# Query splits of layer 2 on VectorE instead of GpSimd, repeated parts copied by ScalarE, and a remade order of steps, in a two-layer transformer kernel

## The chip, the core and the metric

The kernel is one program on one core of a Trainium2 chip. A core has five engines that run their own instruction streams side by side and wait for one another through semaphores: TensorE (PE, matrix products and transposes into PSUM; PEld are its weight loads), VectorE (DVE), ScalarE (ACT), GpSimd (POOL), and SyncE (SP), which here only issues transfers. The metric is the device time of one execution in microseconds, lower is better. The kernel before was timed three times, with a median of 364.91 us (364.82 to 368.45).

## What is computed

Two batches of 512 tokens with 128 features go through a cross attention with a residual, a mixture of experts, a second cross attention, and a block with self attention and gated experts. Cut to what matters here (16 heads of 8 dimensions everywhere; the context has 77 tokens):

```python
x = x + xattn0(layernorm(x), ctx)                 # softmax(q k^T / sqrt(8)) v, projection
x = x + moe0(layernorm(x))                        # 8 experts, top 2: relu(x w1)^2 w2
x = x + xattn1(ctx, layernorm(x))                 # softmax(q k^T) v, + residual, layer norm
# block 2: self attention with rotary q, k over 512 keys
q = rope(src @ Wq); k = rope(src @ Wk_c @ Wk); v = src @ Wv_c @ Wv
x = rmsnorm(src + softmax(q k^T / sqrt(8)) v @ Wo)
shared = swiglu(x @ W_shared_in) @ W_shared_out
routed = sum_e (swiglu(x @ W1_shared) @ W2[e]) * w[:, e]     # grouped top-2 gates
out = rmsnorm(x + shared + routed)
```

## The kernel before

Everything stays in on-chip memory after the loads at the start. Work is cut into steps, written out by hand in one list, `ORDER`. Each engine walks this list and runs its own part of each step, so the list sets the order on every engine at once; what it does not set are the waits, which semaphores enforce. A step's first number is the layer (0 and 1 cross attention, 2 self attention), or, where there is none, the batch.

The steps that matter here:

- `QP`, `KV` and `CKV` project queries and keys. `SPLITQ`, `SPLITK` and `SPLITC` cut each float32 value into three bfloat16 parts (a high part, the rest's high part, and what is left), so that scores can be formed from bfloat16 products without losing accuracy. A row of `qcat` or `kcat` holds six slots of 8 numbers for each head. `Q_PART = (0, 0, 1, 1, 0, 2)` and `K_PART = (0, 1, 0, 1, 2, 0)` say which part stands in which slot: the first part three times, the second twice, the third once. So each split is two casts, two subtractions and three plain copies of a part to its further slots.
- `QT`, `KT` and `KTC` transpose `qcat` and `kcat` on TensorE, and ScalarE or VectorE copies the result out of PSUM (each takes one half of the tokens).
- `SMAX layer group part half` forms scores on TensorE, and VectorE takes their maximum (line 1112). `MCH` splits the maxima (GpSimd in layers 0 and 2, VectorE in layer 1), `MTR` transposes them. `ST` forms the transposed scores less the maximum, and ScalarE takes the exponential (line 896). In layer 1 a further step, the guard, clamps the exponentials (line 545 on GpSimd, line 1120 on VectorE). `PV` is the product with the values, `OC` and `OTR` bring it out.
- `FH` and `FY` are an expert's two products in block 0; `STAT` and `NORM` are normalizations, whose reciprocal root (a power) is always taken by GpSimd; `GH`, `SO`, `RO`, `GT`, `GTE` are the experts and gates of block 2.

PSUM is used as a ring of three large buffers (`ring_ps`), one small one (`misc_ps`) and one for attention outputs (`out_ps`). The ring's buffers are given out in the order of the list, so a step of TensorE waits until the step three places earlier on the ring has been read. `BORROWING` lists small steps that use the ring in place of `misc_ps`.

In layers 0 and 1 and for all keys, the split runs on VectorE (`split`, lines 1016 to 1028). The queries of layer 2 are split by GpSimd (`POOL_SPLITS`, lines 547 to 567), in its own copy of the code and with its own buffer for the rest (`RSP`).

## Time and profile before

| | profile before |
|---|---|
| median of three runs | 364.91 us |
| the profiled execution, its own time | 368.39 us |
| its span, first to last instruction | 366.6 us |
| mean granted TensorE clock | 0.884 of full speed |
| PE busy | 308.5 us (84%) |
| DVE busy | 278.8 us (76%) |
| ACT busy | 203.0 us (55%) |
| POOL busy | 92.0 us (25%) |
| chain that ended last | PE 57%, DVE 21%, issue 10%, ACT 7%, POOL 3% |

The stages follow one another in the span roughly so: loads and the first projections until 20 us, cross attention of layer 0 until 62, experts of block 0 (with the first batch of layer 1 woven in) until 145, the second batch of layer 1 and the first keys and queries of layer 2 until 184, self attention until 305, and the experts of block 2 to the end.

How to read it: an engine's share of busy time is an average over these stages, and in each of them another engine can be the one that the others wait for. The granted clock is the share of its 2.4 GHz that TensorE was given: 1.00 is 2.4 GHz, 0.50 is 1.2 GHz, and a value between is a stretch with some of both. The profiled execution took 3.48 us more than the median.

### The profile page before, as it was taken

How to read it: one execution, taken by the hardware profiler on the slowest of the kernel's cores; microseconds unless marked ns; L12 is line 12 of the kernel's file. 1: busy time of each engine (PE TensorE's matmuls, PEld its weight loads, DVE VectorE, ACT ScalarE, POOL GpSimd, SP SyncE). 2: the span in 40 equal slices, each digit the busy share in tenths (PEclk: the TensorE clock that was granted, in tenths of full speed). 3: DMA queues.
4: the chain of work that ended last, by engine and by line, in shares of the span. 5: the costliest groups of instructions: out<-in, count | busy, mean ns of one | idle time of the engine just before them, and what ended most of it. 6: DMA issues, size and time to landing. Idle time of an engine off the chain costs nothing.

```text
span 366.6 us, 5813 instructions
## 1 busy us (share of the span) xinstructions
PE 308.5 (84%) x2146; PEld 162.5 (44%) x2146; DVE 278.8 (76%) x703; ACT 203.0 (55%) x242; POOL 92.0 (25%) x144
## 2 busy tenths in 40 slices
PE   1679899999998996584877859889889999999990
PEld 0553565577685753572721114242223233745530
DVE  2886667643588968879799699897999851887985
ACT  3245658656664785346452646875779998501200
POOL 4322131010110364319825143911111020011001
PEclk9995889999999999567585587998999999999996
DMA  7910000000000000000000000000000000000000
GB/s 221 431 70 0 2 3 1 2 0 3 0 2 0 2 3 0 0 2 0 2 0 1 3 0 0 2 2 0 2 0 1 2 2 1 0 2 0 30 0 30
DMA packets 1900, 7.48 MB, mean 20 GB/s; under 512 B 208, under 2 KB 336, under 8 KB 1488
## 3 DMA queue, kind: packets, MB, share of 16 engines
q1 hardware_dynamic: 1872, 7.11, 5.2%
q8 instruction: 17, 0.28, 0.3%
q14 instruction: 11, 0.09, 0.1%
HBM read 6.58 MB, written 0.52 MB: 19 GB/s over the span
## 4 chain that ended last, share of the span: by engine, by line
PE 57%; DVE 21%; issue 10%; ACT 7%; POOL 3%; DMA 1%; POOLq 0%; SPq 0%; ACTq 0%; DVEq 0%
PE ring_ps L578 30%; PE out_ps L578 13%; DVE mx L1112 10%; PE ring_ps L674 3%; ACT pT L896 3%; PE misc_ps L578 2%; PE misc_ps L709 2%; ACT qT L880 2%; PE misc_ps L759 1%; ACT hid L924 1%; PE ring_ps L709 1%; DVE Z L960 1%; DVE X L1288 1%; PE misc_ps L595 1%; PE ring_ps L664 1%
## 5 line engine op out<-in xcount | busy, mean ns | idle before, releaser
L896 ACT ACTIVATE pT<-ring_ps 128x1024 f32<-128x1024 f32 (+1 forms) x96 | 94.5, 1025 | 35.3 <-PE ring_ps L578 33.2
L1112 DVE TENSOR_REDUCE mx<-ring_ps 128x2 f32<-128x1024 f32 (+1 forms) x96 | 99.5, 1076 | 13.9 <-PE ring_ps L578 13.1
L506 POOL TENSOR_TENSOR rstd<-var,consts 128x4 f32<-128x4 f32 x14 | 14.7, 1051 | 122.1 <-DVE var L982 62.0
L578 PE MATMUL ring_ps<-XT,f 128*128 128x512 f32 x96 | 44.8, 602 | 0.6 <-ACT hid L924 0.3
L578 PE MATMUL out_ps<-pT,V 128*32 128x512 f32 x256 | 39.8, 666 | 0.0
L545 POOL TENSOR_SCALAR pT<-pT 77x1024 f32<-77x1024 f32 x8 | 23.0, 2880 | 36.4 <-ACT pT L896 36.4
L578 PE MATMUL ring_ps<-f,hid 128*128 128x512 f32 (+1 forms) x96 | 31.8, 487 | 0.0
L578 PEld LDWEIGHTS ring_ps<-f0y,hid 128*128 128x128 f32 x256 | 29.7, 192 | 3.8 <-issue 3.1
L578 PE MATMUL ring_ps<-f0y,hid 128*128 128x128 f32 x256 | 30.9, 277 | 0.1
L578 PE MATMUL ring_ps<-qT,kT 51*128 51x512 bf16 x128 | 24.7, 412 | 6.9 <-DVE mx L1112 3.6
L1288 DVE SCALAR_TENSOR_TENSOR X<-ring_ps,gw,X 128x128 f32<-128x128 f32 x64 | 18.0, 344 | 16.1 <-PE ring_ps L578 15.9
L578 PE MATMUL ring_ps<-kT,qT 48*128 48x512 bf16 x128 | 25.5, 424 | 3.7 <-DVE mx L1112 2.7
L533 POOL TENSOR_SCALAR qcat<-mx 128x16 bf16<-128x16 f32 x16 | 5.3, 330 | 85.9 <-DVE mx L1112 75.8
L578 PEld LDWEIGHTS ring_ps<-XT,f 128*128 128x128 f32 x96 | 17.0, 190 | 18.4 <-issue 15.5
L924 ACT ACTIVATE hid<-ring_ps 128x1024 f32<-128x1024 f32 x16 | 16.3, 1017 | 14.0 <-PE ring_ps L578 14.0
L578 PE MATMUL out_ps<-pT,Vc 77*32 77x512 f32 x128 | 21.7, 720 | 1.6 <-POOL pT L545 1.5
L674 PE MATMUL ring_ps<-identb,qcat 128*128 128x128 bf16 x192 | 17.7, 274 | 5.7 <-DVE qcat L960 5.6
L1288 DVE SCALAR_TENSOR_TENSOR ACC<-ring_ps,gw,ACC 128x128 f32<-128x128 f32 x64 | 19.5, 347 | 3.4 <-PE ring_ps L578 2.4
L578 PEld LDWEIGHTS ring_ps<-f,hid 128*128 128x128 f32 x96 | 15.7, 191 | 14.4 <-issue 14.3
L880 ACT COPY qT<-ring_ps 128x2048 bf16<-128x2048 bf16 x6 | 11.2, 1866 | 18.4 <-PE ring_ps L674 18.4
L578 PE MATMUL ring_ps<-qT,kTc 51*77 51x512 bf16 x64 | 14.5, 485 | 7.0 <-DVE mx L1112 4.4
L674 PEld LDWEIGHTS ring_ps<-identb,qcat 128*128 128x128 bf16 x192 | 16.5, 127 | 7.8 <-DVE qcat L960 6.7
(185 smaller groups left out, 459.1 us busy)
## 6 DMA issues: line engine op xcount, KB each, us to landing
f<-in_f SPq DMA_DIRECT2D x1, 1669.0 KB, 15.2
f<-in_f SPq DMA_DIRECT2D x1, 1028.0 KB, 8.4
f0y<-in_f0y SPq DMA_DIRECT2D x1, 1024.0 KB, 10.4
X<-in_x SPq DMA_DIRECT2D x2, 256.0 KB, 4.5
wb<-in_wb SPq DMA_DIRECT2D x1, 512.0 KB, 11.2
rows<-in_rows SPq DMA_DIRECT2D x1, 512.0 KB, 11.4
trig<-in_trig SPq DMA_DIRECT2D x1, 512.0 KB, 12.0
out<-ACC SPq DMA_DIRECT2D x2, 256.0 KB, 2.0
```

What stands on the lines that cost most here:

```text
L506: return pool.tensor_tensor(out, a, c, op)
L533: pool.tensor_scalar(c[:, :, :, 0], m, -1.0, None, ALU.mult)
L545: pool.tensor_scalar(heads, heads, 0.0, None, ALU.max).then_inc(done["GUARD"], 1)
L578: return nc.tensor.matmul(out, lhsT, rhs, start=start, stop=stop)
L595: last = nc.tensor.transpose(small_ps(step)[:, t * P:(t + 1) * P], source[kind][b][:, t, :], ident)
L674: last = nc.tensor.transpose(ps[:, t, p * P:(p + 1) * P], qcat[b][:, 2 * u + t, p, :], identb[:, :])
L709: last = nc.tensor.transpose(ps[:, a * N + t * P:a * N + (t + 1) * P], qcat[b][:, t, 2 * g + a, :], identb[:, :])
L880: nc.scalar.copy(dst, src).then_inc(ring.read_sem(step), 1)
L896: nc.scalar.activation(probs_buf(layer, i, kt)[0:parts_, 2 * half:2 * half + 2, :], ring_ps[ring.buf(step)][0:parts_, :, :], ACT.Exp, scal ...
L924: nc.scalar.activation(relu[n % 2], src, ACT.Relu).then_inc(ring.read_sem(step), 1)
L1112: V_.tensor_reduce(dst, src, AX.X, ALU.max).then_inc(ring.read_sem(step), 1)
L1288: return V_.scalar_tensor_tensor(out=acc[:, t, :], in0=src, scalar=w, in1=acc[:, t, :], op0=ALU.mult, op1=ALU.add)
```

## The change

- `POOL_SPLITS` is empty: the queries of layer 2 are split by VectorE in the same `split` as all others.
- `split` no longer makes the three copies. It signals after each of its two casts (`PART`), and ScalarE makes the copies in new steps `DUPQ`, `DUPK` and `DUPC`: one instruction of two slots for the first part and one of one slot for the second. There are ten such steps, one for each split. The transposes `QT`, `KT` and `KTC` wait for them as well as for the split.
- `ORDER` and `BORROWING` are written anew. All steps are kept, the ten new ones are put in, and nearly every step stands a few places away from where it was.

```diff
-POOL_SPLITS = {(2, 0), (2, 1)}
+POOL_SPLITS = set()
...
-    STAT n0 0, NORM n0 0, STAT n0 1, XT n0 0, QP 0 0, SPLITQ 0 0, NORM n0 1, CKV 0, SPLITC 0, QT 0 0 0, QT 0 0 1,
+    STAT n0 0, NORM n0 0, CKV 0, SPLITC 0, XT n0 0, QP 0 0, SPLITQ 0 0, DUPQ 0 0, STAT n0 1, DUPC 0, KTC 0 0,
...
             def QT(step, layer, b, u):
 
                 pe.wait_ge(*after("SPLITQ_POOL" if (layer, b) in POOL_SPLITS else "SPLITQ", layer, b))
+                pe.wait_ge(*after("DUPQ", layer, b))
...
+            def copies(split_step, cat, first, heads, part_of, parts=P):
+
+                for k in range(2):
+                    act.wait_ge(*after("PART", *split_step, k))
+                    at = [s for s, part in enumerate(part_of) if part == k]
+                    size = int(np.prod(cat.shape[1:]))
+                    n, gap = len(at) - 1, 3 * DH
+                    out = bass.AP(cat, first * HS + at[1] * DH, [[size, parts], [HS, heads], [gap, n], [1, DH]])
+                    src = bass.AP(cat, first * HS + at[0] * DH, [[size, parts], [HS, heads], [0, n], [1, DH]])
+                    last = nc.scalar.copy(out, src)
+                return last
+
+            def DUPQ(step, layer, b):
+                copies(("SPLITQ", layer, b), qcat[b], 0, T * H, Q_PART).then_inc(done["DUPQ"], 1)
...
-                link(V_.tensor_copy(dst(s0), flat_heads(values)))
+                V_.tensor_copy(dst(s0), flat_heads(values)).then_inc(done["PART"], 1)
+                dve.wait_ge(*after("PART", *step, 0))
                 link(tt(flat_heads(rest), flat_heads(values), dst(s0), ALU.subtract))
-                link(V_.tensor_copy(dst(s1), flat_heads(rest)))
-                for s, k in enumerate(part_of):
-                    if k < 2 and s != (s0, s1)[k]:
-                        V_.tensor_copy(dst(s), dst((s0, s1)[k]))
+                V_.tensor_copy(dst(s1), flat_heads(rest)).then_inc(done["PART"], 1)
+                dve.wait_ge(*after("PART", *step, 1))
                 return tt(dst(s2), flat_heads(rest), dst(s1), ALU.subtract)
```

Three places show what the new list does on an engine. Line numbers of the changed kernel are 6 to 30 higher.

**On TensorE, at the last experts of block 0.** `f0y,hid` is an expert's second product (`FY`), `XT1,f0` its first (`FH`), `qT0,kTc10` the transposed scores of layer 1 (`ST`), `pT,Vc10` the product with the values. Before:

```order
L578 MATMUL ring_ps2<-XT1,f0 128x512 x2
L578 MATMUL out_ps<-pT1,Vc10 32x512 x4
L578 MATMUL ring_ps0<-f0y,hid 128x128 x8
L709 MATMUL misc_ps<-identb,qcat0 128x128 x8
L578 MATMUL ring_ps1<-qT0,kTc10 77x512 x2
L578 MATMUL ring_ps2<-f0y,hid 128x128 x8
L578 MATMUL ring_ps0<-qT0,kTc10 77x512 x2
L578 MATMUL ring_ps1<-wb 128x256
L578 MATMUL ring_ps2<-qT0,kTc10 77x512 x2
L578 MATMUL out_ps<-pT0,Vc10 32x512 x4
```

After the change:

```order
L718 MATMUL ring_ps0<-identb,qcat0 128x128 x8
L584 MATMUL ring_ps1<-XT1,f0 128x512 x2
L584 MATMUL ring_ps2<-f0y,hid 128x128 x8
L584 MATMUL ring_ps0<-qT0,kTc10 77x512 x2
L584 MATMUL out_ps<-pT1,Vc10 32x512 x4
L584 MATMUL ring_ps1<-qT0,kTc10 77x512 x2
L584 MATMUL ring_ps2<-qT0,kTc10 77x512 x2
L584 MATMUL ring_ps0<-f0y,hid 128x128 x8
L584 MATMUL ring_ps1<-qT0,kTc10 77x512 x2
L584 MATMUL out_ps<-pT0,Vc10 32x512 x4
```

The scores of the fourth group, first half (`ST 1 3 0 0`, the row ahead of `wb` before), now stand ahead of the last expert's product instead of behind it, and the transposed maxima (line 709) moved up past two expert products.

**On VectorE, at the first keys and queries of layer 2.** `kcat` and `qcat0` are the split keys and queries, `KF0` and `ACC0` their float32 values, `mx2` and `mx3` maxima of layer 1. Before:

```order
L960 TENSOR_TENSOR KF0<-KF0,Z0 128x512
L1022 CAST kcat<-KF0 128x64x8
L960 TENSOR_TENSOR Z0<-KF0,kcat 128x512
L1024 CAST kcat<-Z0 128x64x8
L1027 COPY kcat<-kcat 128x64x8 x3
L960 TENSOR_TENSOR kcat<-Z0,kcat 128x64x8
L1120 TENSOR_SCALAR pT0<-pT0 77x1024
L1120 TENSOR_SCALAR pT1<-pT1 77x1024
L1112 TENSOR_REDUCE mx3<-ring_ps0 128x2x4
```

After the change:

```order
L991 TENSOR_TENSOR KF0<-KF0,Z0 128x512
L1142 TENSOR_REDUCE mx3<-ring_ps1 128x2x4
L1053 CAST kcat<-KF0 128x64x8
L991 TENSOR_TENSOR Z0<-KF0,kcat 128x512
L1056 CAST kcat<-Z0 128x64x8
L991 TENSOR_TENSOR kcat<-Z0,kcat 128x64x8
L1053 CAST qcat0<-ACC0 128x64x8
L991 TENSOR_TENSOR Z0<-ACC0,qcat0 128x512
L1056 CAST qcat0<-Z0 128x64x8
L991 TENSOR_TENSOR qcat0<-Z0,qcat0 128x64x8
L1150 TENSOR_SCALAR pT0<-pT0 77x1024
L1121 COPY kT0<-ring_ps1 128x2x8x128
```

The three copies are gone, the four operations of the query split came in, one maximum moved ahead of both, and the second guard moved behind.

**On TensorE, at the first products with the values of layer 2.** `kT0,qT0` are scores for the maxima (`SMAX`), `qT0,kT0` the transposed ones (`ST`), `pT,V0` the products with the values (`PV`). Before:

```order
L578 MATMUL ring_ps2<-qT0,kT0 128x512 x2
L578 MATMUL ring_ps0<-qT0,kT0 128x512 x2
L578 MATMUL out_ps<-pT0,V0 32x512 x4
L578 MATMUL out_ps<-pT1,V0 32x512 x4
L578 MATMUL ring_ps1<-kT0,qT0 128x512 x2
L578 MATMUL ring_ps2<-kT0,qT0 128x512 x2
```

After the change:

```order
L584 MATMUL out_ps<-pT1,Vc11 32x512 x4
L584 MATMUL ring_ps0<-kT0,qT0 128x512 x2
L584 MATMUL ring_ps1<-qT0,kT0 128x512 x2
L584 MATMUL ring_ps2<-qT0,kT0 128x512 x2
L584 MATMUL out_ps<-pT0,V0 32x512 x4
L584 MATMUL ring_ps0<-kT0,qT0 128x512 x2
L584 MATMUL ring_ps1<-qT0,kT0 128x512 x2
L584 MATMUL out_ps<-pT1,V0 32x512 x4
```

Scores for the maxima now stand between the first two products with the values; before, both products stood ahead of the next such score.

## Rows read from the trace of the kernel before

**Rows 1.** Busy time by stretch: us; busy and count by engine; granted clock; DMA.

```profile
145.00:168.00 23.00, 15.59 (x138) 12.66 (x138) 19.21 (x55) 10.64 (x19) 6.37 (x7) 0.63 0.00 1
...
168.00:184.00 16.00, 10.40 (x94) 7.75 (x94) 13.64 (x28) 7.86 (x7) 13.84 (x8) 0.57 0.00 1
...
188.00:212.00 24.00, 17.64 (x80) 3.72 (x80) 20.13 (x39) 12.31 (x15) 8.74 (x9) 0.57 0.00 1
...
225.00:268.00 43.00, 38.22 (x302) 14.38 (x298) 38.46 (x45) 32.62 (x34) 14.74 (x22) 0.96 0.00 1
...
268.00:305.00 37.00, 35.49 (x265) 11.33 (x266) 28.34 (x45) 33.00 (x37) 4.86 (x16) 1.00 0.00 1
...
305.00:356.00 51.00, 51.00 (x186) 25.92 (x184) 39.11 (x147) 14.09 (x17) 2.01 (x2) 1.00 0.02 6
...
sum 366.60, PE 308.48 PEld 162.45 DVE 278.76 ACT 203.01 POOL 92.00; mean PE 25.71 PEld 13.54 DVE 23.23 ACT 16.92 POOL 7.67
```

**Rows 2.** Timeline, 136.9 to 145: start us, duration, engine, what, [idle before].

```profile
136.92 2.05 PE L578 MATMUL ring_ps<-f0y,hid 128*128 128x128 f32 x16
...
140.51 2.76 POOL L545 TENSOR_SCALAR pT<-pT 77x1024 f32<-77x1024 f32 x1 [3.58 <-ACT pT L896]
...
141.88 0.16 DVE L978 TENSOR_SCALAR var<-mv 128x4 f32<-128x4 f32 x1
...
143.25 1.46 POOL L506 TENSOR_TENSOR rstd<-var,consts 128x4 f32<-128x4 f32 x1
...
145.02 1.65 ACT L844 ACTIVATE XN<-X,shift,rstd 128x128 f32<-128x128 f32 x4 [3.05 <-POOL shift L506]
```

**Rows 3.** Groups of VectorE and ScalarE instructions by line and shape.

```profile
L1027 DVE COPY qcat<-qcat 128x512 bf16<-128x512 bf16 x12 | 3.7, 367 | 0.1
...
L1027 DVE COPY kcat<-kcat 128x512 bf16<-128x512 bf16 x6 | 2.5, 468 | 0.1
...
L1027 DVE COPY kcat<-kcat 77x256 bf16<-77x256 bf16 x6 | 1.0, 219 | 0.1
...
L1022 DVE CAST qcat<-ACC 128x512 bf16<-128x512 f32 x4 | 1.7, 424 | 0.1
...
L1022 DVE CAST kcat<-KF 128x512 bf16<-128x512 f32 x2 | 1.2, 606 | 0.0
...
L960 DVE TENSOR_TENSOR Z<-ACC,qcat 128x512 f32<-128x512 f32 x4 | 2.8, 692 | 0.1
...
L888 ACT COPY qT<-misc_ps 128x1024 bf16<-128x1024 bf16 x14 | 14.1, 1008 | 7.2 <-PE misc_ps L709 7.2
...
L908 ACT COPY oT<-out_ps 128x512 f32<-128x512 f32 x16 | 9.4, 588 | 7.1 <-PE out_ps L578 6.9
```

**Rows 4.** Timeline, 172 to 184: keys and queries of layer 2, batch 0.

```profile
172.37 1.52 DVE L1027 COPY kcat<-kcat 128x512 bf16<-128x512 bf16 x3
...
174.39 1.71 POOL L506 TENSOR_TENSOR qcat<-RSP,qcat 128x512 bf16<-128x512 f32 x1
...
177.50 1.87 PE L664 MATMUL ring_ps<-identb,kcat 128*128 128x128 bf16 x16 [1.07 <-DVE mx L1112]
...
179.16 3.62 PE L674 MATMUL ring_ps<-identb,qcat 128*128 128x128 bf16 x32
...
182.82 1.22 DVE L1099 COPY qT<-ring_ps 128x2048 bf16<-128x2048 bf16 x1 [1.45 <-PE ring_ps L674]
```

**Rows 5.** Timeline, 210.6: VectorE's longest wait in layer 2.

```profile
210.57 8.01 DVE L1112 TENSOR_REDUCE mx<-ring_ps 128x2 f32<-128x1024 f32 x7 [3.23 <-PE ring_ps L578]
```

**Rows 6.** Timeline, 238 to 245: queries of layer 2, batch 1.

```profile
238.65 1.15 POOL L506 TENSOR_TENSOR qcat<-RSP,qcat 128x512 bf16<-128x512 f32 x1
...
241.89 1.07 PE L674 MATMUL ring_ps<-identb,qcat 128*128 128x128 bf16 x16
...
243.00 1.87 ACT L880 COPY qT<-ring_ps 128x2048 bf16<-128x2048 bf16 x1 [1.77 <-PE ring_ps L674]
```

**Rows 7.** Timeline, 357: the last sums of experts.

```profile
357.25 2.55 DVE L1288 SCALAR_TENSOR_TENSOR ACC<-ring_ps,gw,ACC 128x128 f32<-128x128 f32 x8 [0.89 <-PE ring_ps L578]
```

More of the change, by code:

```diff
@@ L381, in after @@
                 return done[kind], same.index(("OTR",) + args) + 1
+            if kind == "PART":
+                on_pool = args[:1] == ("SPLITQ",) and args[1:3] in POOL_SPLITS
+                same = [s for s in splits if (s[0] == "SPLITQ" and s[1:] in POOL_SPLITS) == on_pool]
+                return done["PARTP" if on_pool else "PART"], 2 * same.index(args[:-1]) + args[-1] + 1
             if kind == "QROT":
@@ L397, in build @@
         hidden = [s[1:] for s in schedule if s[0] == "FH"]
+        splits = [s for s in schedule if s[0] in ("SPLITQ", "SPLITK", "SPLITC")]
         maxes = [s[1:3] for s in schedule if s[0] == "SMAX" and s[3:] == (0, 0)]
@@ L560, in SPLITQ @@
                 s0, s1, s2 = (Q_PART.index(k) for k in range(3))
-                link(copy(dst(s0), values))
+                copy(dst(s0), values).then_inc(done["PARTP"], 1)
+                pool.wait_ge(*after("PART", *step, 0))
                 link(tt(rest, values, dst(s0), ALU.subtract))
-                link(copy(dst(s1), rest))
-                for s, k in enumerate(Q_PART):
-                    if k < 2 and s != (s0, s1)[k]:
-                        copy(dst(s), dst((s0, s1)[k]))
+                copy(dst(s1), rest).then_inc(done["PARTP"], 1)
+                pool.wait_ge(*after("PART", *step, 1))
                 tt(dst(s2), rest, dst(s1), ALU.subtract).then_inc(done["SPLITQ_POOL"], 1)
@@ L651, in KTC @@
                 pe.wait_ge(*after("SPLITC", layer))
+                pe.wait_ge(*after("DUPC", layer))
                 wait_free(ring, step)
@@ L659, in KT @@
                 pe.wait_ge(*after("SPLITK", b))
+                pe.wait_ge(*after("DUPK", b))
                 wait_free(ring, step)
@@ L1015, in CKV, with split @@
                 last.then_inc(misc.read_sem(step), 1)
-            def split(cat, first, pairs, values, rest, part_of, parts=P):
+            def split(step, cat, first, pairs, values, rest, part_of, parts=P):
                 def dst(s):
@@ L1033, in SPLITC @@
                 flatr = kr[0:C, :, :].rearrange("p b d -> p (b d)")
-                split(kcat, 2 * layer * H, B * H, flatk, flatr, K_PART, C).then_inc(done["SPLITC"], 1)
+                split(step, kcat, 2 * layer * H, B * H, flatk, flatr, K_PART, C).then_inc(done["SPLITC"], 1)
             def rotate(src, out, tmp):
```

114 lines of the change are left out of this document (60 added, 54 removed).

## Prediction

> **What bounds the kernel now.** I read the busy time by stretch first [rows 1], since the shares of the whole span mix stages. TensorE is busy for 308.48 of 366.60 us, but not evenly. From 305 to 356 us it is busy for all 51.00, and from 268 to 305 for 35.49 of 37, at a granted clock of 1.00. There the end is set by TensorE's work, and no other engine's relief helps. From 145 to 212 it is different. Between 168 and 184 TensorE is busy for 10.40 of 16 us while VectorE is busy for 13.64, and between 188 and 212 for 17.64 of 24 against VectorE's 20.13. The granted clock in both is 0.57, that is mostly 1.2 GHz, after stretches in which TensorE waited. So the middle of the kernel is paced by VectorE and by waits, and it costs twice, once as idle time and once as a slow clock. A change of this kind must earn its time there.
>
> Second came the timeline around the hand-over from block 0 to layer 1 [rows 2]. GpSimd clamps exponentials from 140.51 to 143.27, and the statistics that it should turn into the reciprocal root were ready at 142.04 (141.88 and 0.16). The root starts at 143.25, the normalization that hangs on it at 145.02. All work of the second batch of layer 1 follows from it.
>
> Third, the prices of the operations that move [rows 3], and fourth, the two places where the queries of layer 2 are made [rows 4, 6].
>
> **The change, part by part.**
>
> *Copies taken off VectorE.* The 24 copies of a part are 3.7, 2.5 and 1.0 us of VectorE, 7.2 in all [rows 3]. For one query split that is 3.7/4 = 0.9 us. A further gain is indirect: the cast of keys takes 606 ns and that of queries 424 for the same shape. The keys of layer 2 are cast while GpSimd works on the queries, so I put the difference down to that, and it goes with the GpSimd split. It is 0.18 us for each cast.
>
> *Query splits put on VectorE.* Each is two casts and two subtractions, 2 x 0.424 + 2 x 0.692 = 2.2 us [rows 3], so 4.4 us for two. VectorE thus does 7.2 - 4.4 = 2.8 us less in all, plus some tenths.
>
> *Copies put on ScalarE.* The trace has no copy within SBUF on this engine. The nearest rows are its copies out of PSUM, 1.01 us for 1024 elements and 0.59 for 512 [rows 3]. A query or key pair is one of each, so 1.6 us. Six query pairs and two key pairs are 12.8 us, and the two context pairs about 1.6 us more (0.6 and a little less for half of it): some 14 us. From below I take the 512-element price for both (9.4 us for the eight), from above 3 us for a pair if the short runs of 8 elements cost double. I take 1.6, since the rows have the same size and type.
>
> The Trainium skill, "ScalarE: Activation LUTs" (Rules for kernel authors), says plain elementwise operations belong on VectorE, which is up to about 3 times faster for one source in bf16. The trace agrees with its direction, and by it the trade is a loss wherever ScalarE is the one waited for. That is the slower rival below.
>
> *Layer 0.* On the path of a split, ScalarE's second copy can start after the second cast and ends (0.59) with VectorE's last subtraction (0.69), so where ScalarE is free the transposes start 0.9 us earlier. In the experts' stage TensorE covers it. In layer 0 I take 0.9 us for one of the two batches (the other's copies stand behind exponentials and context copies). **-0.9**, bounds 0 and -1.8.
>
> *The root behind the clamp.* The new order puts those scores ahead of the last expert product of 2.05 us, so the clamp ends before the statistics are ready, and the root can start at 142.04 instead of 143.25 [rows 2]. **-1.2**, bounds 0 (if the exponentials ahead of it are late) and -2.05.
>
> *Keys and queries of layer 2, batch 0.* VectorE loses the key copies (1.52 us here [rows 4]) and 0.36 for slower casts, and gains 2.2, net +0.3. GpSimd ends the split at 176.10, but TensorE takes up these transposes only at 179.16, because it is busy with the keys' until 179.37 [rows 4]. So GpSimd's slowness was hidden, and taking it away gains nothing by itself. The keys could start earlier now. But ScalarE's two pairs (3.2 us) are waited for; it is busy for only 7.86 of 16 us there [rows 1], so they fit. **0**, bounds -1.5 (the copies that went) and +2.2.
>
> *VectorE's wait of 3.23 us before 210.57* [rows 5]. It comes from two products with the values in a row, with no scores for a maximum between them. The new order puts scores there. But exponentials, products and transposed maxima now stand together a little later, and there VectorE may wait anew. I take half, **-1.6**, bounds 0 and -3.23.
>
> *Keys and queries of layer 2, batch 1.* Here GpSimd ends at 239.80 and TensorE starts the transposes at 241.89 [rows 6], so again it was hidden. VectorE's sum is even (+2.2, -1.25, some tenths). ScalarE gets two pairs in a row, 3.2 us, ahead of its two transposed halves of 1.87. It is busy for 32.62 of 43 us here and 33.00 of 37 right behind [rows 1]. Behind the copies wait the exponentials, behind these the products with the values, and TensorE for a free ring buffer. It idles for 10.4 us in the stretch, so most is absorbed. **+1.0**, bounds 0 and +3.2.
>
> *The end.* The second batch's gates come later in the new order. VectorE now waits 0.89 us before the last experts' sums [rows 7], so lateness up to that is free. **+0.2**, bounds 0 and +1.0. The silu steps move between exponentials, but the number of table loads stays at four, and TensorE has its own work beside them.
>
> The sum is -0.9 - 1.2 + 0 - 1.6 + 1.0 + 0.2 = -2.5 us. The profiled execution took 368.39, so it would take 365.9. It lay 3.48 above the median of 364.91, which therefore goes to **362.4 us**. All bounds at once would be 364.91 - 8.6 = 356.3 and 364.91 + 6.4 = 371.3.
>
> **The rivals.**
>
> *The clock holds (0.20).* The sum leaves TensorE's clock as it was. In 168 to 184 and 188 to 212 TensorE is busy for 28.0 us at 0.57 [rows 1]; at 1.00 this work would take 12.0 us less (28.0 x 0.43). For it speaks that both the longest wait of VectorE and the wait for the root go, and with them some of TensorE's idle time ahead of these stretches. Against it speaks that VectorE is busy for 20.13 of 24 us, so a faster TensorE mostly waits for it. A third of 12.0 gives -4, and with the sum above **358.4 us**. The Trainium skill, "TensorE: Matmul & The Clock Gate" (Part 1), says that the clock is throttled by default and released by activity. The trace agrees: 1.00 in the dense stretch behind 268, 0.57 in the two with waits.
>
> *Nothing comes of it (0.18).* The GpSimd split was hidden in both batches [rows 4, 6], and each new order trades one wait for another. Then VectorE's waits come back a few steps later, and the time is **365 us**, between 363.5 and 366.5.
>
> *ScalarE becomes the bound (0.22).* The mechanism is the queue at the keys and queries of layer 2: two pairs of copies there, 3.2 us in each batch, stand ahead of transposed halves and exponentials, so that TensorE stalls for a ring buffer. It decides if the idle time of ScalarE near the copies is less than the 3.2 us that they take, though the stretch as a whole has 10.4. With both pairs paid in full and the wait before 210.57 not gained the sum is -0.9 - 1.2 + 3.2 + 3.2 + 0.2 = +4.5, so **369.4 us**. For it speaks that ScalarE is busy for 33.00 of 37 us behind the second place. Against it: half the time idle at the first.
>
> **How the numbers follow.** The forecast above has 0.40, with a range of its own from 360.0 to 364.6. A measurement of this kernel can tell about 1% from no change, that is below 361.3 or above 368.6. Faster by over 1%: the clock's 0.20, and 0.18 of the forecast's 0.40, 0.38 in all. Slower by over 1%: most of ScalarE's 0.22, 0.20. The rest, 0.42, is no change: 0.22, 0.18 and 0.02. For 8 in 10 the range must reach to the clock's case and into ScalarE's: 356.3, where all bounds at once lie, is more than needed, so 356.5 to 369.0.
>
> **What would show it.** In the profile of the changed kernel:
> - ScalarE's copies within SBUF at about 1.0 and 0.6 us, ScalarE near 217 us busy, VectorE near 275, and GpSimd's 92.00 us down by its two splits.
> - The root behind the last clamp starts within 0.3 us of its statistics. If it waits for the clamp again, the term of -1.2 is wrong.
> - VectorE's longest wait for scores in layer 2 is under 2 us. If one of 3 us stands elsewhere, the term of -1.6 is wrong.
> - Exponentials right behind the copies of batch 1 wait for ScalarE itself and TensorE idles for under 1 us there. If it idles for 3, the slower rival holds.
> - The granted clock between 145 and 228 stays near 0.6. If it is above 0.8, the clock's rival holds.
>
> The prediction as a whole is wrong if TensorE's idle time in layers 1 and 2 grows, or if a place that I did not look at, such as layer 0 with its new order, changes by more than 2 us.

## The result and the profile after

The changed kernel takes 366.69 us (median of 20 executions) against 364.91 for the one before (20, on the same chip). Their ratio is 1.0052, with a 95% interval from 1.0033 to 1.0071. It is slower, by about half a per cent, where 362.4 was forecast. The range of 356.5 to 369.0 holds it.

All ratios below compare a kernel with the one before on the same chip. 0.1% is 0.365 us, and "+1.9 us" for a ratio of 1.0052 is worked out so. The ratios are not those of the medians and leave out executions over 1.5% above the fastest of their kernel, so the two can differ by up to 1.8 us (e1: +5.3 by the ratio, +7.1 by the medians).

The page of the changed kernel: busy time by engine, then the granted clock in 40 slices, in tenths.

```profile
span 365.7 us, 5806 instructions
...
PE 305.4 (84%) x2146; PEld 160.4 (44%) x2146; DVE 273.6 (75%) x687; ACT 217.1 (59%) x262; POOL 70.7 (19%) x130
...
PEclk9978999999999996667675589999899999999997
```

ScalarE has 14.1 us more, as forecast (217), and VectorE 5.2 less, where 275 would have been 3.8 less. The span is 0.9 us shorter than the one shown of before, although the medians say 1.8 longer. That execution of before lay 3.48 above its median, this one 0.78. A second profile of the unchanged kernel (below) serves as the comparison.

Busy time by stretch, columns as in [rows 1]:

```profile
20.00:62.00 42.00, 37.19 (x408) 21.83 (x406) 30.90 (x72) 29.41 (x41) 12.57 (x43) 0.92 0.01 5
...
145.00:168.00 23.00, 13.54 (x136) 11.00 (x136) 19.02 (x43) 11.10 (x17) 3.54 (x6) 0.68 0.00 1
168.00:184.00 16.00, 11.78 (x108) 8.56 (x108) 12.45 (x24) 10.87 (x11) 3.27 (x2) 0.68 0.00 1
...
188.00:212.00 24.00, 19.31 (x92) 3.66 (x92) 20.50 (x30) 9.22 (x10) 5.85 (x9) 0.53 0.00 1
...
225.00:268.00 43.00, 36.91 (x288) 14.61 (x288) 38.64 (x47) 33.16 (x38) 3.83 (x15) 0.96 0.00 1
268.00:305.00 37.00, 36.03 (x251) 12.79 (x250) 27.92 (x47) 32.16 (x36) 4.81 (x16) 1.00 0.01 1
305.00:356.00 51.00, 50.23 (x192) 24.34 (x190) 38.75 (x145) 13.97 (x16) 2.02 (x2) 1.00 0.02 6
```

Against [rows 1] the middle looks alike: TensorE idles for 9.5 us from 145 to 168 (7.4 before), and its clock from there to 212 is 0.53 to 0.68 in the long stretches. The rival in which the clock holds did not come about. The end is TensorE's as before.

The root behind the clamp, timeline at 132 to 140 (to be held against [rows 2]):

```profile
131.99 6.02 POOL L552 TENSOR_SCALAR pT<-pT 77x1024 f32<-77x1024 f32 x2 [2.90 <-ACT pT L926]
...
136.91 0.16 DVE L1009 TENSOR_SCALAR var<-mv 128x4 f32<-128x4 f32 x1
...
137.98 1.46 POOL L513 TENSOR_TENSOR rstd<-var,consts 128x4 f32<-128x4 f32 x1
...
139.75 1.65 ACT L853 ACTIVATE XN<-X,shift,rstd 128x128 f32<-128x128 f32 x4 [2.23 <-POOL shift L513]
```

The statistics are ready at 137.07 and the root starts at 137.98, right behind a clamp that ends at 138.01. It waits 0.91 us, where it waited 1.21.

Keys and queries of layer 2, batch 0 (against [rows 4]):

```profile
166.18 1.03 ACT L926 ACTIVATE pT<-ring_ps 77x1024 f32<-77x1024 f32 x1
...
167.30 2.77 POOL L552 TENSOR_SCALAR pT<-pT 77x1024 f32<-77x1024 f32 x1 [14.10 <-ACT pT L926]
167.34 1.28 DVE L1053 CAST kcat<-KF 128x512 bf16<-128x512 f32 x1
168.65 1.04 ACT L878 COPY kcat<-kcat 128x1024 bf16<-128x1024 bf16 x1 [1.43 <-DVE kcat L1053]
...
169.38 0.97 DVE L1056 CAST kcat<-Z 128x512 bf16<-128x512 f32 x1
170.38 0.62 ACT L878 COPY kcat<-kcat 128x512 bf16<-128x512 bf16 x1 [0.69 <-DVE kcat L1056]
...
171.13 3.59 PE L672 MATMUL ring_ps<-identb,kcat 128*128 128x128 bf16 x32 [4.36 <-DVE kcat L991]
...
175.03 1.94 PE L584 MATMUL out_ps<-pT,Vc 77*32 77x512 f32 x8
...
176.90 3.41 PE L683 MATMUL ring_ps<-identb,qcat 128*128 128x128 bf16 x32
...
180.35 1.22 DVE L1129 COPY qT<-ring_ps 128x2048 bf16<-128x2048 bf16 x1 [2.34 <-PE ring_ps L683]
```

GpSimd's split is gone, but one of its clamps now lies beside VectorE's casts of the keys. They take 1.28 and 0.97 us, where I had counted 0.42 for each. TensorE idles 4.36 us for the keys. ScalarE's copies have the forecast prices, 1.04 and 0.62. The new list also has a product with the values (175.03) ahead of the queries' transposes, where the old list has it behind them, and VectorE waits 2.34 us for these.

Batch 1, ScalarE's queue (against [rows 6]):

```profile
235.61 4.70 ACT L926 ACTIVATE pT<-ring_ps 128x1024 f32<-128x1024 f32 x5
240.14 1.60 ACT L878 COPY qcat<-qcat 128x1024 bf16<-128x1024 bf16 x2
241.59 1.61 ACT L878 COPY kcat<-kcat 128x1024 bf16<-128x1024 bf16 x2
...
241.84 1.95 PE L683 MATMUL ring_ps<-identb,qcat 128*128 128x128 bf16 x32 [1.73 <-ACT qcat L878]
...
243.06 1.92 ACT L910 COPY qT<-ring_ps 128x2048 bf16<-128x2048 bf16 x1
...
243.83 1.23 DVE L1129 COPY qT<-ring_ps 128x2048 bf16<-128x2048 bf16 x1 [1.53 <-PE ring_ps L683]
```

The parts of the queries were ready at 238.78 (a cast of 0.43 from 238.35), but ScalarE reached the first copy only at 240.14, behind five exponentials in a row. It makes four copies in 3.06 us. TensorE idles 1.73 us for those of the queries, between the 1 and the 3 that the prediction had named as signs, and VectorE then waits 1.53 for the transposes.

VectorE's waits from 180 to 250, in all, times, longest:

```profile
DVE mx L1142 <- PE ring_ps L584: 4.6, 6, 2.1
DVE qT L1129 <- PE ring_ps L683: 3.9, 2, 2.3
DVE oT L1185 <- PE out_ps L584: 1.1, 2, 0.8
```

The wait of 3.23 [rows 5] is gone, and in its place stand six waits for scores of 4.6 us together, and 3.9 for queries. The last sums of experts [rows 7] start at 356.32 with a wait of 0.53.

Ends of steps on VectorE, from the traces (us). Below, *early* is up to the statistics of layer 2's first input, *batch 0* from there to the last copied query of layer 2's batch 0, *batch 1* to the first maximum of group 4 in layer 2, *end* the rest. "Last row" is the end of VectorE's last operation:

| kernel | statistics | batch 0 queries | group 4 | last row | early | batch 0 | batch 1 | end |
|---|---|---|---|---|---|---|---|---|
| before, second profile | 156.48 | 183.09 | 249.23 | 361.22 | 156.5 | 26.6 | 66.1 | 112.0 |
| after | 151.82 | 181.57 | 250.75 | 363.17 | 151.8 | 29.8 | 69.2 | 112.4 |

So the changed kernel is 4.7 us ahead at layer 2's statistics, gives back 3.1 at batch 0 and 3.0 at batch 1, and loses 0.4 at the end. These are two single executions; the medians say 1.8, these say 1.95.

### The profile page after: what moved, and what is told of

Read it like the earlier page. It is cut to its first block, busy times and chain, and to the rows that moved or that the text cites. A ratio compares the mean times of both kernels' runs of the same rounds, so it can differ in the third digit from the quotient of the medians.

```text
span 365.7 us, 5806 instructions
## 1 busy us (share of the span) xinstructions
PE 305.4 (84%) x2146; PEld 160.4 (44%) x2146; DVE 273.6 (75%) x687; ACT 217.1 (59%) x262; POOL 70.7 (19%) x130
## 4 chain that ended last, share of the span: by engine, by line
PE 57%; DVE 20%; issue 10%; ACT 8%; POOL 3%; DMA 1%; POOLq 0%; SPq 0%; ACTq 0%; DVEq 0%
PE ring_ps L584 28%; PE out_ps L584 12%; DVE mx L1142 10%; PE ring_ps L683 4%; PE misc_ps L584 4%; ACT pT L926 3%; POOL pT L552 2%; PE ring_ps L718 2%; PE ring_ps L672 2%; PE misc_ps L768 1%; DMA wa<-in_wa 1%; DVE Z L991 1%; PE misc_ps L718 1%; ACT qcat L878 1%; PE misc_ps L601 1%
## 5 line engine op out<-in xcount | busy, mean ns | idle before, releaser
L926 ACT ACTIVATE pT<-ring_ps 128x1024 f32<-128x1024 f32 (+1 forms) x96 | 94.8, 1024 | 29.7 <-PE ring_ps L584 25.3
L584 PE MATMUL ring_ps<-XT,f 128*128 128x512 f32 x96 | 43.9, 598 | 0.0
L584 PE MATMUL out_ps<-pT,V 128*32 128x512 f32 x256 | 38.6, 651 | 0.0
L584 PE MATMUL ring_ps<-kT,qT 48*128 48x512 bf16 x128 | 26.4, 437 | 5.4 <-DVE mx L1142 3.8
L683 PE MATMUL ring_ps<-identb,qcat 128*128 128x128 bf16 x192 | 16.2, 260 | 7.6 <-DVE qcat L991 4.6
L584 PEld LDWEIGHTS ring_ps<-kT,qT 48*128 48x128 bf16 x128 | 5.9, 96 | 31.7 <-issue 13.7
L683 PEld LDWEIGHTS ring_ps<-identb,qcat 128*128 128x128 bf16 x192 | 15.1, 121 | 10.4 <-issue 5.3
L959 ACT ACTIVATE hid<-hid 128x1024 f32<-128x1024 f32 x16 | 16.9, 1057 | 3.1 <-PE ring_ps L584 2.7
```

The source lines that it names most:

```text
L584: return nc.tensor.matmul(out, lhsT, rhs, start=start, stop=stop)
L683: last = nc.tensor.transpose(ps[:, t, p * P:(p + 1) * P], qcat[b][:, 2 * u + t, p, :], identb[:, :])
L926: nc.scalar.activation(probs_buf(layer, i, kt)[0:parts_, 2 * half:2 * half + 2, :], ring_ps[ring.buf(step)][0:parts_, :, :], ACT.Exp, scal ...
L959: nc.scalar.activation(h2[n % 2][:, :, :].rearrange("p c n -> p (c n)"), relu[n % 2], ACT.Square).then_inc(done["FH"], 1)
```

## The experiments

Ratios, intervals and medians (e0 has one execution, 365.51 us). "Old" and "new" order are those of before and of the changed kernel. *Early* covers layers 0 and 1 up to the query transposes of layer 1's second batch (`QT 1 1 1`).

| | early: order, copies | layer 2: order, splits of queries, copies | median | ratio to before (95%) |
|---|---|---|---|---|
| before | old, VectorE | old, GpSimd, with the split | 365.4 | 1 |
| e4 | old, ScalarE | old, GpSimd, with the split | 366.57 | 1.0037 (1.0011 to 1.0063) |
| e2 | old, ScalarE | old, GpSimd, ScalarE | 371.23 | 1.0186 (1.0147 to 1.0224) |
| e1 | old, ScalarE | old, VectorE, ScalarE | 372.54 | 1.0146 (1.0100 to 1.0192) |
| e3 | new, VectorE | new, GpSimd, with the split | 371.74 | 1.0153 (1.0115 to 1.0192) |
| e10 | new, ScalarE | new, GpSimd, with the split | 371.01 | 1.0129 (1.0077 to 1.0180) |
| e5 | new, ScalarE | new, VectorE, VectorE | 365.33 | 1.0000 (0.9966 to 1.0034) |
| after | new, ScalarE | new, VectorE, ScalarE | 366.69 | 1.0052 (1.0033 to 1.0071) |
| e6 | new, ScalarE | as the changed kernel, one clamp more on VectorE | 368.53 | 1.0073 (1.0039 to 1.0107) |
| e11 | new, VectorE | old, GpSimd, with the split | 363.83 | 0.9937 (0.9897 to 0.9977) |
| e7 | new, ScalarE | old, GpSimd, with the split | 361.99 | 0.9914 (0.9882 to 0.9946) |
| e15 | the same again | | 361.75 | 0.9905 (0.9873 to 0.9938) |
| e12 | new, ScalarE | old; batch 0 as e7; batch 1 VectorE, VectorE | 362.01 | 0.9899 (0.9859 to 0.9939) |
| e14 | new, ScalarE | old; as e7, batch 0's key copies ScalarE | 361.48 | 0.9856 (0.9796 to 0.9917) |
| e8 | new, ScalarE | old, VectorE, VectorE | 364.40 | 0.9980 (0.9947 to 1.0013) |
| e16 | new, ScalarE | old, VectorE; copies: batch 0 ScalarE, 1 VectorE | 362.31 | 0.9918 (0.9889 to 0.9946) |
| e17 | new, ScalarE | old; batch 0 as e7; batch 1 VectorE, ScalarE | 365.58 | 1.0019 (1.0003 to 1.0035) |
| e9 | new, ScalarE | old, VectorE, ScalarE | 366.52 | 0.9995 (0.9960 to 1.0031) |
| e13 | new, ScalarE | old, VectorE, ScalarE, batch 0 behind exponentials | 366.68 | 1.0023 (0.9983 to 1.0064) |

### The two halves of the change: e0 to e3

e0 is the kernel before, unchanged.

> The kernel before, unchanged, for a second profile of it. The first one was 368.39 us where the median is 364.91, and its granted clock from 20 to 62 us was 0.80. If the clock of a single execution makes this gap, this execution lies near 365 us, its clock in that stretch is nearer to 0.9, and VectorE's busy time is the same 276 us within 1.

It took 365.51 us, with a clock of 0.84 from 20 to 62 us instead of 0.80. So 2.9 of the 3.48 us by which the first profile lay high were that one execution. They are not lost in that stretch: at the statistics of layer 2's first input the two profiles are 0.1 us apart. They arise behind it, where the granted clock from 145 to 305 us was 0.84 instead of 0.81.

e1 has the old list with the new steps put in. The second query split had to be moved up, since VectorE would otherwise wait for its own later step.

```diff
-    MTR 1 5, SPLITK 0, SPLITQ 2 0, ST 1 4 0 0, ST 1 4 0 1, ST 1 5 0 0, ST 1 5 0 1, SMAX 1 7 0 0, SMAX 1 7 0 1, KT 0 0,
+    MTR 1 5, SPLITK 0, DUPK 0, SPLITQ 2 0, DUPQ 2 0, ST 1 4 0 0, ST 1 4 0 1, ST 1 5 0 0, ST 1 5 0 1, SMAX 1 7 0 0,
...
-    PV 2 1 3, SPLITK 1, SMAX 2 3 0 1,
+    PV 2 1 3, SPLITK 1, DUPK 1, SPLITQ 2 1, DUPQ 2 1, SMAX 2 3 0 1,
```

> The order and the borrowed buffers of before, with both engine changes: the query splits of layer 2 on VectorE and all copies of parts on ScalarE, each right behind its split. Theory A (the engine change gains, the remade order loses): 363 to 364 us, 0.3 to 0.5% under the kernel before. Theory B (the copies queued on ScalarE at the keys and queries of layer 2 cost more than GpSimd's relief gives, and the remade order only repairs that): 367 to 369 us. Theory C (neither matters, waits trade places): 365 within 0.7.

e2 is the same with GpSimd's splits kept (`DUPQ 2 1` then stands behind `KT 1 1`):

```diff
-POOL_SPLITS = set()
+POOL_SPLITS = {(2, 0), (2, 1)}
```

> The order of before, copies of parts on ScalarE, but the query splits of layer 2 still on GpSimd. It holds one half of the engine change alone. Theory A: near 364.5, since the GpSimd split was hidden and only the copies matter, and they are taken off VectorE (-0.9 in layer 0). Theory B: 366 to 368, since the queue of copies on ScalarE is all there. Theory C: 365 within 0.7.

e3 is the kernel before with the new list and borrowed buffers, without the `DUP` steps.

> The remade order and borrowed buffers, with the engines of before: query splits of layer 2 on GpSimd, copies of parts on the engine that splits. Theory A (the order loses): 367 to 369 us, more than the changed kernel's 366.7. Theory B (the order gains about 1 to 2 by the root and the wait of 3.23 us): 363 to 364. Theory C: 365 within 0.7. In layer 2 VectorE now has the copies within a queue laid out without them, so up to 1.5 us more than this at each of the two places is possible under all three.

Each half alone costs 1.5%, 5.3 us for both engine changes in the old order (e1) and 5.6 for the order (e3); the copies alone, without VectorE's query splits, cost 6.8 (e2). Order and engines together cost 0.5%. Theory B was right in kind on the copies, though they cost more than it said (+6.8 in e2), and wrong on the order. A was right on the order and wrong on the engines. The new order is laid out for a quick query split, and with GpSimd's VectorE waits 5.2 us for those queries (e3, VectorE's waits from 170 to 192):

```profile
DVE qT L1098 <- PE ring_ps L673: 5.2, 1, 5.2
```

### Where each part pays: e4 to e7

e4 has ScalarE's copies in layers 0 and 1 only. `DVE_COPIES` names the splits that make their own copies as before:

```diff
+DVE_COPIES = {('SPLITK', 1), ('SPLITQ', 2, 0), ('SPLITQ', 2, 1), ('SPLITK', 0)}
...
                 dve.wait_ge(*after("PART", *step, 1))
+                if step in DVE_COPIES:
+                    for s, k in enumerate(part_of):
+                        if k < 2 and s != (s0, s1)[k]:
+                            V_.tensor_copy(dst(s), dst((s0, s1)[k]))
```

> The order of before; copies of parts on ScalarE in layers 0 and 1 only. Layer 2 stays as in the kernel before: its query splits on GpSimd, its copies behind the splits on the engine that splits. Theory Q (the copies queue ahead of exponentials at the keys and queries of layer 2; in the trace of the kernel with all copies on ScalarE in this order VectorE's step lay 3.6 us later behind the first place and 3.2 behind the second): nearly all of that kernel's +5.8 us is there, so this one lies within 1.5 us of before, 364.0 to 367.0 us. Theory R (the loss is the clock or layers 0 and 1): 369 us or more.

+1.4 us, against +6.8 with layer 2's copies on ScalarE too. So in the old order 5.4 of the 6.8 are layer 2's. Theory Q holds.

e5 is the changed kernel with the same `DVE_COPIES` and without layer 2's four `DUP` steps.

> The changed kernel, with the copies of layer 2's parts (four pairs of keys and queries) put back on VectorE behind their splits; query splits stay on VectorE, copies of layers 0 and 1 on ScalarE. Theory Q (ScalarE's queue is what costs in the changed kernel too): 364 to 366 us, faster than its 366.7, since 6.4 us of ScalarE go and 5 us of VectorE come at places where ScalarE was queued. Theory O (the new order is fitted to ScalarE's copies, and VectorE is on the path there): about 1 us for each of the four pairs, 369 to 371 us.

1.9 us less than the changed kernel. The intervals touch, so it points to Q and rules out O's 369 to 371. In its profile batch 0, batch 1 and end (as in the table of steps) are 28.5, 68.8 and 111.2 us, against 29.8, 69.2 and 112.4 in the changed kernel. So of its gain only 0.4 us lies in batch 1.

e6 puts one clamp on VectorE:

```diff
-DVE_GUARDS = {(i, 1) for i in range(NGRP)}
+DVE_GUARDS = {(i, 1) for i in range(NGRP)} | {(4, 0)}
```

> The changed kernel, one clamp more on VectorE: the first half of layer 1's group 4, which GpSimd clamps from 167.30 to 170.07 us while VectorE casts the keys. The casts took 1.28 and 0.97 us there, against 0.42 without GpSimd beside them. Theory P (a running GpSimd operation slows VectorE's casts): both casts take 0.4 to 0.5 us, the keys' split is 1.4 us shorter, VectorE pays 0.68 for the clamp, and the kernel gains 0.5 to 1, 365.7 to 366.3 us. Theory N (casts are slow there for another reason): the casts stay above 0.9 and the kernel is 0.7 slower, 367.4.

368.53 us, 1.0073 (1.0039 to 1.0107), not told apart from the changed kernel's 1.0052. The casts, in its timeline:

```profile
168.47 0.69 DVE L1149 TENSOR_SCALAR pT<-pT 77x1024 f32<-77x1024 f32 x1 [0.73 <-ACT pT L925]
...
169.78 0.41 DVE L1052 CAST kcat<-KF 128x512 bf16<-128x512 f32 x1
...
170.96 0.43 DVE L1055 CAST kcat<-Z 128x512 bf16<-128x512 f32 x1
```

Theory P is right on the cause: without GpSimd beside them the casts take 0.41 and 0.43. It is wrong on the gain: the 1.41 us saved equal what VectorE spends on the clamp (0.69) and on its wait for the exponential (0.73). So the slow casts alone do not account for what the changed kernel loses.

e7 is a splice: the changed kernel's list and copies up to `QT 1 1 1`, from there the old list, with `POOL_SPLITS` and layer 2's copies as before.

> Layers 0 and 1 up to the queries of layer 1's second batch in the new order, with ScalarE's copies; from there on the order, the borrowed buffers and the engines of before. The changed kernel led a plain execution of before by 4.7 us at this place and lost it later. Theory L (the lead is real and the old second part keeps it): 361 to 363 us, the fastest of all. Theory G (the lead is given back anyway, since the second part then waits for TensorE at its low clock or for another engine): 364.5 to 366.

361.99 us: the lead is real and the old second part keeps it. The changed kernel's loss lies behind `QT 1 1 1`. e15, the same kernel in a later comparison, confirms it with 361.75.

### Layer 2, part by part, on e7: e8 to e12

e8 empties `POOL_SPLITS` in e7; VectorE splits and copies, and the second query split is moved up as in e1.

> As the kernel with layers 0 and 1 new and the rest old (361.99 us), but layer 2's query splits on VectorE, with their copies behind them on VectorE. Theory H (GpSimd's split was hidden, VectorE is what is waited for in this stretch): two splits with copies are 2 x 3.1 us of VectorE, from which the slowed casts of the keys give back some 1 us, so 364.5 to 367 us. Theory W (the GpSimd split was waited for): 360.5 to 362.

e9 also gives the copies to ScalarE, right behind the splits (`SPLITK 0, DUPK 0, SPLITQ 2 0, DUPQ 2 0`).

> As the kernel of 361.99 us, but with both engine changes in layer 2 too: query splits on VectorE, copies on ScalarE right behind the splits, in the old order of that part. Theory Q (ScalarE's queue costs 3.2 us at each of the two places; the same change cost 4.7 to 6 us in the old order): 366 to 369 us. Theory Z (it only looked so because layers 0 and 1 were laid out for other engines): 361 to 363.

e10 is the changed kernel with `POOL_SPLITS` and layer 2's copies as before.

> The changed kernel's whole order, ScalarE's copies in layers 0 and 1, but the engines of before in layer 2: its query splits on GpSimd, copies behind the splits. Against the kernel of 361.99 us it differs by the order from layer 1's second batch on alone. Theory F (the new order of layer 2 is laid out for a quick split: VectorE waited 5.17 us for queries where all engines were those of before): 369 to 371 us, near the 371.74 of that kernel. Theory S (the new order of layer 2 is simply worse by what is missing between 361.99 and 365.33): 365 to 367.

e11 is e7 with all copies on VectorE.

> Layers 0 and 1 in the new order and the rest in the old one, all engines as before. Against the kernel of 361.99 us it has the copies of layers 0 and 1 on VectorE. Theory V (the lead of 4.7 us in layers 0 and 1 comes from the new order; ScalarE's copies add little): 361.5 to 363 us. Theory K (it comes from ScalarE's copies, which take 0.9 us off VectorE for each query split): 364 to 366.

Early part: the order alone gives -2.3 us (e11), ScalarE's copies with it -3.1 to -3.5 (e7, e15). The difference of about 1 us is not told apart, so V is favoured over K, no more. Layer 2: moving both query splits to VectorE costs 2.4 us (e8 against e7), H; with ScalarE's copies it is 3.0 (e9), less than Q's 3.2 at each of two places. e10 confirms F. Against e10, e5 differs in `POOL_SPLITS` alone and is 4.7 us faster: in the new order VectorE's split gains what it loses in the old one, and more.

From e7 three single changes lead to the changed kernel: the query splits to VectorE (e8, +2.4 us), the new order behind `QT 1 1 1` (e5, +0.7), the copies to ScalarE (+1.9). They add up to the 5.0 by which the changed kernel lies above e7. The middle one is within the intervals.

At batch 0 of e8 a clamp of GpSimd starts where its split was, and VectorE pays beside it:

```profile
164.54 5.69 POOL L552 TENSOR_SCALAR pT<-pT 77x1024 f32<-77x1024 f32 x2 [12.02 <-ACT pT L933]
```

```profile
164.69 1.43 DVE L998 TENSOR_TENSOR Z<-KF,kcat 128x512 f32<-128x512 f32 x1
...
166.62 2.23 DVE L1068 COPY kcat<-kcat 128x512 bf16<-128x512 bf16 x3
...
169.37 1.13 DVE L1060 CAST qcat<-ACC 128x512 bf16<-128x512 f32 x1
...
171.73 0.70 DVE L1068 COPY qcat<-qcat 128x512 bf16<-128x512 bf16 x3
```

Three copies of the same size take 2.23 us while GpSimd works and 0.70 after it has stopped at 170.23. Not every operation beside it is slowed: a cast at 166.15 takes 0.43 us there, and the subtraction at 168.77 takes 0.68. [rows 3] had 0.37 us for one copy as a mean over both cases.

e12 is e8 with the first split back on GpSimd, `POOL_SPLITS = {(2, 0)}`.

> As the kernel of 361.99 us, but layer 2's second query split (batch 1) on VectorE with its copies; the first one stays on GpSimd. With both on VectorE the time was 364.40, and in its profile VectorE's step behind the first split lay 3.4 us later and stayed so to the end, while of the 3 to 4 us behind the second one most was taken back by a wait of 1.30 that vanished. Theory D (the first place costs, the second is nearly free): 361.5 to 363 us. Theory E (both cost alike, half of 2.4 each): 363.2.

362.01 us, so theory D: the second split, moved up in the list, is free on VectorE, and the first one bears the whole cost (e8 against e12, 3.0 us by the ratios).

### Which of ScalarE's copies cost: e13, e16, e17, e14

e13 changes only the place of two steps in e9:

```diff
-    MTR 1 5, SPLITK 0, DUPK 0, SPLITQ 2 0, DUPQ 2 0, ST 1 4 0 0, ST 1 4 0 1, ST 1 5 0 0, ST 1 5 0 1, SMAX 1 7 0 0,
+    MTR 1 5, SPLITK 0, SPLITQ 2 0, ST 1 4 0 0, ST 1 4 0 1, ST 1 5 0 0, ST 1 5 0 1, DUPK 0, DUPQ 2 0, SMAX 1 7 0 0,
```

> As the kernel with old order and both new engines in layer 2 (366.52 us), but ScalarE makes the copies of batch 0's keys and queries behind the four exponentials of layer 1's groups 4 and 5 instead of ahead of them. In that kernel the exponentials began at 169.21 us, 5.9 later than in the kernel of 361.99, and TensorE idled 4.22 for them. Theory Q (the place in ScalarE's queue is what costs): exponentials start near 164.3 again, the keys' transposes at about 170, 2.5 to 3 us are won, 363.5 to 364.5. Theory X (ScalarE's work or VectorE's split cost wherever they stand): 366 to 367.

In the profile of e9 the exponentials and TensorE behind them wait for ScalarE:

```profile
169.21 3.74 ACT L925 ACTIVATE pT<-ring_ps 77x1024 f32<-77x1024 f32 x4
170.27 0.65 PE L583 MATMUL ring_ps<-qT,kTc 51*77 51x512 bf16 x2 [4.22 <-ACT pT L925]
```

In that of e13 they start at 165.41, and batch 0, taken as in the table of steps, is 26.8 instead of 29.6 us. Yet the ratios are 1.0023 and 0.9995, no gain. Q was right that the exponentials move up, and wrong on the time.

e16 takes e13 and gives batch 1's copies back to VectorE; e17 has ScalarE's copies at batch 1 only.

> Old order behind layers 0 and 1, the first query split of layer 2 on VectorE and batch 0's copies on ScalarE behind the four exponentials, as in the kernel of 366.68 us; at batch 1 the split is on VectorE too but its copies of keys and queries are VectorE's. Measured so far: the kernel with batch 0 as before and this batch 1 took 362.01. In the profile of the one of 366.68 batch 0 came out even (0.1 us) and batch 1 lost 2.2. Theory B1 (the copies on ScalarE at batch 1 cost, those at batch 0 nothing once they stand behind the exponentials): 361.5 to 363.5 us. Theory B0 (the profile of one execution misled, and batch 0 costs): 365 to 367.

> The counterpart: batch 0 of layer 2 as before (query split on GpSimd, copies with the splits), batch 1 with its query split on VectorE and its copies of keys and queries on ScalarE right behind the splits. Theory B1: 364.5 to 367 us, since two pairs of copies, 3.2 us, stand there ahead of transposed halves and exponentials. Theory B0: 361.5 to 363.

e16: 362.31 us, as fast as e12. e17: 365.58, 4.4 us more than e12 by the ratios, with intervals apart. (Its profile is of an execution of 386.35 us and is not read.) Theory B1 holds: in the old order ScalarE's copies at batch 0 cost nothing where they stand behind the exponentials, and those at batch 1 cost about 4 us, which e13 pays too (3.8 more than e16). Whether the copies at batch 0 would cost ahead of the exponentials is not shown: no run has them there with batch 1's on VectorE.

What happens there shows in two timelines at batch 1. e16, copies on VectorE:

```profile
229.27 4.69 ACT L933 ACTIVATE pT<-ring_ps 128x1024 f32<-128x1024 f32 x5 [0.63 <-PE ring_ps L588]
...
230.44 0.70 DVE L1068 COPY kcat<-kcat 128x512 bf16<-128x512 bf16 x3
...
233.40 1.06 PE L678 MATMUL ring_ps<-identb,kcat 128*128 128x128 bf16 x16
```

e13, copies on ScalarE:

```profile
228.91 4.69 ACT L925 ACTIVATE pT<-ring_ps 128x1024 f32<-128x1024 f32 x5 [0.63 <-PE ring_ps L583]
...
233.44 1.59 ACT L877 COPY kcat<-kcat 128x1024 bf16<-128x1024 bf16 x2
234.89 1.60 ACT L877 COPY qcat<-qcat 128x1024 bf16<-128x1024 bf16 x2
...
235.13 1.70 PE L671 MATMUL ring_ps<-identb,kcat 128*128 128x128 bf16 x16 [1.94 <-issue]
...
237.41 1.23 DVE L1141 TENSOR_REDUCE mx<-ring_ps 128x2 f32<-128x1024 f32 x1 [2.77 <-PE ring_ps L583]
```

VectorE has both casts of the keys' parts done at 230.04, but ScalarE is in a run of exponentials and reaches the copies at 233.44. TensorE idles 1.94 us, for which the profile names no other engine, and starts the keys' transposes at 235.13, right behind the end of the keys' copies at 235.03; the next scores stand behind these on TensorE, and VectorE waits 2.77 us for them. In e16 the same copies were 0.70 us of VectorE, and the transposes started 1.7 us earlier in an execution that was 0.4 us later by its exponentials. VectorE's longest wait from 225 to 250 is 1.1 us there.

e14 is e7 with batch 0's key copies on ScalarE behind the four exponentials.

> As the kernel of 361.99 us, but the copies of batch 0's key parts in layer 2 (1.52 us of VectorE, between 166.35 and 167.87) are made by ScalarE behind the same four exponentials, where it idled for 3.42 us. Theory Y (VectorE's keys are what TensorE waits for there, and ScalarE is free): the second copy ends near VectorE's last subtraction, the transposes of the keys start 1.0 to 1.5 us earlier, 360.5 to 361.3 us. Theory M (ScalarE's exponentials end at 167.0, so the copies end no earlier than VectorE's did): 362 within 0.5.

361.48 us, 0.9856 (0.9796 to 0.9917). It has the lowest ratio of all, but its interval holds e7, e12 and e15, and by the medians it is 1.1% under before, as e15 is 1.0% and e12 0.9%. So Y and M are not told apart. e7, e12, e14 and e16 beat both kernels by about 1%.

## Why the prediction was wrong

Against the second profile of before, the steps forecast and found are: early -2.1 and -4.7 us, batch 0 none and +3.1, batch 1 (the wait and the copies together) -0.6 and +3.0, end +0.2 and +0.4. The early gain came. The prediction failed in layer 2, where it took batch 0 as even and batch 1 as a small gain, and this turned -2.5 into +1.9.

**Layer 0 (-0.9) and the root (-1.2), together -2.1.** The early part gave -3.1 to -3.5 by the ratios (e7, e15), and the profiles show a lead of 4.7. The root's share is at most 0.3: the clamp is earlier, but so is the root, and they meet again. So the total is of the right size and the term of the root is wrong. At the root's statistics 4.4 of the 4.7 are already there (137.07 us against 141.42), and 2.6 at the first statistics of block 0 (55.20 against 57.82), where I had looked at one term. The prediction had named a change of over 2 us in such a place as a sign against itself. Part of the 2.6 may belong to the execution and not to the kernel. Twelve profiles share these steps word for word. In seven, the changed kernel's among them, the point lies at 54.4 to 55.4 us, in five (e6, e10, e13, e14, e15) at 56.5 to 57.0. The clock granted from 20 to 40 us is 0.83 or 1.00 in the seven and 0.64 to 0.66 in the five, but for e10 with 1.00; in the second profile of before it is 0.69. So the ratios are the safer figure, and what makes the lead was not separated further.

**Keys and queries, batch 0 (0).** In the old order the move of the split costs 3.0 us (e8 against e12), and with ScalarE's copies behind the exponentials that cost is gone (e16), so 0 was attainable. In the changed kernel it was not: 3.1 us of lead are gone here. The step that failed is "it goes with the GpSimd split", on the slow casts. GpSimd's work beside the casts did not go, a clamp took its place, and the casts took 2.25 us instead of 0.84. How the 3.1 divide is not shown: e6 took the 1.41 of the casts away and was not faster, the wait of 2.34 behind a product with the values was tested by no run, and e5, with VectorE's copies, is 1.2 shorter here.

**The wait of 3.23 (-1.6).** It went as forecast and came back as others. The condition in the prediction, "there VectorE may wait anew", is what happened. The profiles price the new order in this stretch, *batch 1*:

| order behind `QT 1 1 1` | batch 1: split, copies | kernels | stretch, us |
|---|---|---|---|
| old | GpSimd, with the split | e7, e14, e15 | 66.9 |
| old | VectorE, VectorE | e8, e12, e16 | 66.8 to 67.1 |
| old | VectorE, ScalarE | e13, e9 | 69.0, 70.6 |
| new | VectorE, VectorE | e5 | 68.8 |
| new | VectorE, ScalarE | changed kernel | 69.2 |

With the same engines the new order costs 2.0 us here, where -1.6 was forecast. This is the step that failed most in the changed kernel, as far as one profile each of it and of e5 can say. Over the whole kernel less is left of it (e5 against e8 +0.7; the changed kernel against e9 and e13 +2.1 and +1.1 by the ratios, 0.8 and 0.5 by the medians), which these intervals do not tell from nothing throughout.

**Batch 1 (+1.0).** In the old order this term measured about +4 (e17 less e12, e13 less e16), above my upper bound of 3.2. The mechanism was named right, the queue on ScalarE. I wrote that "most is absorbed" since TensorE idles for 10.4 us in the stretch. But a sum over 43 us says nothing of the 6 us in which the copies fall: ScalarE had five exponentials in a row ahead of them. And I priced what ScalarE takes, 3.2, not the delay until it takes it, 3.4 us from 230.04 to 233.44 in e13. VectorE's own sum was no "even" either: 2.2 less 1.25 is +0.95, less some tenths. In the new order the price is smaller: e5 is 1.9 faster with the copies of both batches on VectorE, and only 0.4 of that lies in this stretch of the profiles. The two costs do not add up: the stretch takes about 69 us with the new order, with ScalarE's copies (e13; 70.6 in e9), or with both.

**What the copies save (-7.2 on VectorE).** The sum of VectorE's busy time was near (-3.8 to the forecast 275, -5.2 measured), the value was not. Without GpSimd beside them three copies cost 0.70 us, 0.23 for each, where I had taken 0.37 (the mean of [rows 3], slowed ones included). At batch 1 that is two times 0.70 on VectorE against 3.06 to 3.2 on ScalarE. The Trainium skill, "ScalarE: Activation LUTs" (Rules for kernel authors), puts plain elementwise operations on VectorE as up to about 3 times faster in bf16. For these copies the ratio is 1.60/0.70 = 2.3, and the trade lost about 4 us at batch 1 of the old order and 1.9 in the new one, both batches together.

**The end (+0.2).** It measured 0.4 us in the profile (112.4 against 112.0). Right.

**The rivals.** The time came out as in "nothing comes of it" (363.5 to 366.5) and a little above, but not by its mechanism alone: the early gain was lost again in layer 2. "ScalarE becomes the bound" had the size by luck: 3.2 at each of the two places, where the profiles show 3.1 and 3.0. With the early part at -4.7 instead of -2.1 its sum is 364.9 - 4.7 + 3.2 + 3.2 + 0.2 = 366.8. Its cause holds for batch 1 of the old order. In the changed kernel, moving the copies back to VectorE gains only 1.9 (e5), of the 5.0 by which it lies above e7; the query splits had cost 2.4 of these (e8). The clock did not hold (0.53 to 0.68).

What stays open: why e9 and e13 are alike in time though their batch 0 differs by 2.8 us in the profile. A single execution is not enough here. e16 has e13's batch 0 word for word and took 28.6 us for it instead of 26.8, with a granted clock of 0.66 instead of 0.74 from 160 to 180. In two profiles of e7 and e15, the same kernel, the step at layer 2's statistics ends at 150.84 and 153.48.

## What to carry to other kernels

Before handing work to an engine with idle time, read the 5 us around the place, not the stretch: what stands ahead in its queue when the input is ready is part of the price, not only the work's own duration. An order tuned by hand and the assignment of engines belong together; here each half of the change alone cost about three times what both cost, and a splice at one step, with the new list ahead of it and the old one behind, was faster than either. When an engine is relieved so that another runs undisturbed, look at what moves up into its place.
